# Deformable window sums: one product instruction and one matmul batch per slot, where there were two of each

## The chip, the cores and the metric

The program runs on one core of a Trainium2 chip. The metric is the device time of that core in microseconds (us), the median of several executions. Lower is better.

## The reference, cut to what matters

The kernel is a chain of four layers on an input of 16 images, 64 channels and 16x16 pixels, each added back to its input: a focal modulation block (L0), a deformable convolution (L1), a graph layer over 4,096 nodes (L2) and a convolution with binary weights (L3). The change lies in the deformable convolution alone:

```python
value = (xf @ vp_w.T + vp_b).reshape(n, L, G, cg)      # 8 groups of 8 channels
...
sampled = gather(y0i, x0i, (1 - ty) * (1 - tx)) + gather(y0i, x0i + 1, (1 - ty) * tx) \
        + gather(y0i + 1, x0i, ty * (1 - tx)) + gather(y0i + 1, x0i + 1, ty * tx)
out = jnp.einsum('nhwgk,nhwgkc->nhwgc', mask, sampled)
out = out.reshape(n, L, c) @ op_w.T
```

Offsets are small, so each output pixel needs values from a window of 5x5 pixels. The kernel computes, for each of the 25 window positions (a *slot*), a weight per pixel and group, and sums weight times shifted value over the slots. A path for offsets that reach beyond the window stands behind a flag and isn't taken here.

## The kernel before, in words

Partitions hold image and group and column (or channel and group, in other stages), the free dimension holds pixels (PX = 256). All is in float32 in this stage.

The window stage has four kinds of work, on three engines.

- *Folds* (GpSimd, `fold_rows`, L617, and one of VectorE's, L1128). They multiply the hat functions of y and x for one of nine pairs of window row and tap row into a buffer of nine maps, in three instructions of 768 elements each. Order: pairs 2, 1, 3, then 4, 5, 6 interleaved, then 7, 8. Five buffers; a pair that reuses a buffer waits until the slots of the window row that read it are built (`slot_ready`). Between them GpSimd masks hats (L607).
- *Slot builds* (TensorE, `build_slots`, `add_term`, L1504). They sum the fold maps of a slot, shifted by a constant matrix, into one of four slots in PSUM banks 4 to 7, with 64x64 matmuls of 256 columns. A group of two slots is built at once, in two stages. The group of slots 16 and 17 needs the 18th fold.
- *Products* (VectorE, L1151). For each slot the weights in PSUM times the shifted values in SBUF, once for channels 0, 1, 4, 5 of the layout and once for 2, 3, 6, 7: two instructions (`hh`) of 4 x n elements a partition. n is 224, 240 or 256 pixels, by the window row (slots 0 to 9: 224; 10 to 14 and 20 to 24: 240; 15 to 19: 256). Each goes to one of five ring buffers of 1,024 columns, and waits until the sum that read the buffer is done (`window_added`).
- *Accumulations* (TensorE, `accumulate`, L1490). For each half of a slot, 16 matmuls of 32x32 (4 partition quarters by 4 outputs) with n columns, each with a shift matrix as weights, add the products to banks 0 to 3. A bank holds 256 columns of either half. I call these 16 matmuls a batch.

TensorE's order is written out: the builds of groups 0 and 1, then for each group k the accumulations of its two slots and the build of group k+2. The last group is slot 24 alone. All engines wait on semaphores and run their own streams in order. Ahead of the stage TensorE makes the 27 maps (`pointwise`, L1352) and VectorE turns them (`turn_maps`, L1116). `chunk_of` says which channel lies where, and rules the order in which the weights of the output projection are loaded (`raw2`) and the copy out of the path that isn't taken.

Of the kernel before, what the change touches and what calls it, by code (L numbers as in the profile page):

```python
# [28 lines left out]
P = 128  # L29
# [15 lines left out]
def bass_preact_convs(nc, x, toep3, toep5, toep7, toepd, pw0, pw1, pw2, bias_n, small_x, key_b,  # L45
# [4 lines left out]
    with ctx:  # L50
# [8 lines left out]
        def dram(t, off, dims):  # L59
            return bass.AP(t.tensor, t.offset + off, [list(d) for d in dims])  # L60
# [46 lines left out]
        def cut(lo, n):  # L107
            assert lo + n <= ARENA
            return arena[:, lo:lo + n]
# [38 lines left out]
        dN = turns[:, 0:FULL]  # L148
        omN = [turns[:, FULL:2 * FULL], turns[:, 2 * FULL:3 * FULL]]

        ring = [turns[:, 2304 + c * 1024:3328 + c * 1024] for c in range(3)] + [cut(19968, 1024), cut(6912, 1024)]
        RING, SLOTS, ROW = len(ring), 25, 5
        GROUPS = [(s, s + 1) for s in range(0, 24, 2)] + [(24,)]
        A = sb("A", 3 * PX)

# [58 lines left out]

        def chunk_of(i, j):

            return 4 * ((i ^ j) // 2) + (i ^ j) % 2

        def terms(s, swapped):

# [94 lines left out]
        def slow_vector(dve):  # L315
# [67 lines left out]
            for i in range(4):  # L383
                for j in range(4):
                    ins = dve.tensor_scalar(view(ps, i * 512, [(PX, 2), (1, PX)], 32 * j, 32),
                                            view(acc, chunk_of(i, j) * PX, [(2 * PX, 2), (1, PX)], 32 * i, 32), 1.0, None,
                                            ALU.mult)
            ins.then_inc(sem("window_sum"), 1)
            dve.wait_ge(sem("window_sum"), 1)
# [40 lines left out]
        @block.sync  # L430
        def _(sp):
            load_images(sp, (0, 1), 0)
            load_images(sp, (0, 1), 1)
            load_images(sp, (0, 1), 2)
            load_images(sp, (0, 1), 3)
            sp.dma_start(band5, dram(toep5, 0, [(640, P), (1, 640)])).then_inc(sem("band5_in"), 16)
            sp.dma_start(sN, dram(bias_n, 0, [(13, 32), (0, 4), (1, 13)])).then_inc(sem("bias_in"), 16)
            sp.wait_ge(sem("wt_zero"), 1)
            bands(sp, wt3, toep3, 3, "wt3_in")
            sp.wait_ge(sem("wt_zero"), 2)  # L440
            bands(sp, wt7, toep7, 7, "wt7_in")
            sp.dma_start(sX, dram(small_x, 0, [(SX_N, 8), (0, 16), (1, SX_N)])).then_inc(sem("smallx_in"), 16)
            sp.wait_ge(sem("keyb_zero"), 1)
            sp.dma_start(keyb[0:64, :], dram(key_b, 0, [(0, 64), (1, 1)])).then_inc(sem("small_in"), 16)
            sp.dma_start(rowN[0:16, :], dram(row_n, 0, [(0, 16), (1, 12)])).then_inc(sem("small_in"), 16)
            sp.dma_start(v2raw[0:32, :], dram(v2_w, 0, [(8, 8), (64, 4), (1, 8)])).then_inc(sem("small_in"), 16)
            for gp in range(2):
                for c4hi in range(2):
                    sp.dma_start(view(turned_x, SX_N * c4hi, [(1, SX_N)], 64 * gp, 64),
                                 dram(small_x, 4 * c4hi * SX_N, [(SX_N, 4), (0, 16), (1, SX_N)])  # L450
                                 ).then_inc(sem("turned_in"), 16)
            for p, row in turned_rows:
                sp.dma_start(raw1[p:p + 16, :], dram(pw1, row * 640, [(640, 4), (0, 4), (1, 640)])
                             ).then_inc(sem("raw1_in"), 16)
            for c in range(2):
                sp.dma_start(rawv[:, 64 * c:64 * c + 64],
                             dram(pw1, 256 + 320 * c, [(640, 32), (0, 4), (1, 64)])).then_inc(sem("rawv_in"), 16)
            sp.wait_ge(sem("wt_zero"), 3)
            bands(sp, wtd, toepd, 3, "wtd_in")
            sp.dma_start(alphaT[:, :], dram(alpha, 0, [(0, 2), (1, 64)])).then_inc(sem("l3_in"), 16)  # L460
            sp.dma_start(wraw, dram(sign_w, 0, [(0, 2), (576, 64), (1, 576)])).then_inc(sem("l3_in"), 16)
            for swap, t in enumerate(bias_rows):
                for c4 in range(C4):
                    sp.dma_start(t[32 * c4:32 * c4 + 32, :], dram(bias_n, (c4 ^ (2 * swap)) * 104, [(0, 32), (1, 104)])
                                 ).then_inc(sem("map_bias_in"), 16)
            for j in range(4):
                for i in range(4):
                    p, row = 32 * j + 8 * i, 8 * i + chunk_of(i, j)
                    sp.dma_start(raw2[p:p + 8, :], dram(pw2, row * 128, [(2 * 128, 2), (0, 4), (1, 128)])
                                 ).then_inc(sem("raw2_in"), 16)  # L470

            sp.wait_ge(sem("x2_ready"), 2)
            sp.wait_ge(sem("x2_kept"), 2)
            for c4 in range(C4):
                sp.dma_start(nat(scratch_x2, c4), quad(xs, c4)).then_inc(sem("x2_out"), 16)
            sp.wait_ge(sem("x2_out"), 64)

            sp.dma_start(x2R, dram(scratch_x2, 0, [(64, P), (8192, 32), (1, 64)])).then_inc(sem("x2R_in"), 16)

            sp.wait_ge(sem("HM"), 4)  # L480
            sp.wait_ge(sem("MH"), 4)
            for t in (HM, MH):
                sp.dma_start(t[:, 4096:6144], t[:, 0:2048]).then_inc(sem("wrap_in"), 16)
            for i, q in enumerate((2, 3, 0, 1)):
                sp.wait_ge(sem("y_ready"), i + 1)
                sp.dma_start(dram(out, q * 65536, [(PX, P), (32768, 2), (1, PX)]),
                             view(yout, q * 512, [(PX, 2), (1, PX)])).then_inc(sem("y_out"), 16)
            sp.wait_ge(sem("y_out"), 64)
# [416 lines left out]
        def _(dve):  # L905
# [213 lines left out]
            turn_maps(0, 0)  # L1119
            turn_maps(0, 1)  # L1120
            turn_maps(1, 0)
            for hh in range(2):
                dve.memset(view(ring[hh], 0, [(PX, 4), (1, 2 * HW)]), 0.0).then_inc(sem("ring_zero"), 1)
            turn_maps(1, 1)
            turn_maps(2, 0)
            dve.wait_ge(sem("masked"), 1)
# [8 lines left out]
            for p in range(SLOTS):  # L1135
                by = ROWS[p // ROW]
                if p == 12:
                    dve.wait_ge(sem("over"), 2)
                    dve.tensor_reduce(oversum, over[:, 0:2], AX.X, ALU.add).then_inc(sem("over_rows"), 1)
                dve.wait_ge(sem("slot_ready"), p + 1)  # L1140
                if p == 21:
                    dve.wait_ge(sem("over_all"), 1)
                    dve.tensor_scalar(flag[0:1, :], bank(5)[0:1, PX:PX + 1], 0.0, None, ALU.is_gt).then_inc(sem("flag"), 1)
                y0, n, dy = inside(by)
                for hh in range(2):
                    m = 2 * p + hh
                    if m == RING - 1:
                        dve.wait_ge(sem("maps_turned"), 16)
                    if m >= RING:
                        dve.wait_ge(sem("window_added"), m - RING + 1)  # L1150
                    dve.tensor_tensor(out=view(ring[m % RING], y0, [(512, 2), (PX, 2), (1, n)]),  # L1151
                                      in0=view(values_x, 2 * hh * PX + y0 + dy, [(4 * PX, 2), (PX, 2), (1, n)]),
                                      in1=view(slot(p), y0, [(0, 2), (0, 2), (1, n)]), op=ALU.mult).then_inc(sem("window_prod"), 1)
            dve.wait_ge(sem("flag"), 1)
            far = dve.value_load(flag[0:1, 0:1], min_val=0, max_val=1)
            dve.wait_ge(sem("window_added"), 2 * SLOTS)
            with dve.If(far == 1):
                dve.wait_ge(sem("folded"), 3 * (len(FOLDS) - 1))
                slow_vector(dve)
# [188 lines left out]
        def _(pe):  # L1348
# [130 lines left out]
            values(1)  # L1479
            pe.wait_ge(sem("dw_bias"), G)  # L1480

            def accumulate(p, hh):

                bx = p % ROW
                pe.wait_ge(sem("window_prod"), 2 * p + hh + 1)
                w = ident if bx == 2 else shift[bx]
                y0, n, _ = inside(ROWS[p // ROW]) if p else (0, PX, 0)
                for j in range(4):
                    for i in range(4):
                        ins = pe.matmul(view(bank(i), hh * PX + y0, [(1, n)], 32 * j, 32),  # L1490
                                        view(w, 32 * i, [(1, 32)], 32 * i, 32),
                                        view(ring[(2 * p + hh) % RING], PX * (i ^ j) + y0, [(1, n)], 32 * i, 32),
                                        start=(p == 0 and hh == 0), stop=(p == SLOTS - 1 and hh == 1))
                ins.then_inc(sem("window_added"), 1)

            def add_term(s, i, swapped, n, begins):
# [47 lines left out]
            build_slots(0)  # L1544
            build_slots(1)
            pe.wait_ge(sem("maps_turned"), 16)
            pe.wait_ge(sem("ring_zero"), 2)
            for k, group in enumerate(GROUPS):
                for p in group:
                    accumulate(p, 0)  # L1550
                    accumulate(p, 1)
                if 17 in group:
                    pe.wait_ge(sem("over_rows"), 1)
                    pe.matmul(bank(5)[0:1, PX:PX + 1], oversum, ones[:, 0:1], start=True, stop=True).then_inc(sem("over_all"), 1)
# [226 lines left out]
```

## Time and profile before

| what | us |
|---|---|
| median of 3 executions | 313.93 |
| lowest and highest | 312.32, 315.7 |
| span of the profiled execution | 310.8 |
| between median and span | 3.1 |

The span runs from the first to the last instruction of the program; the time of an execution also takes in what lies around it. The time of the profiled execution itself isn't told beside its span, so the difference to the median stands for it. PE is TensorE, PEld its weight loads, DVE VectorE, ACT ScalarE, POOL GpSimd. A matmul in float32 leaves two records and two weight loads in the trace. Ends of matmuls are modelled, so their starts are the safer reading.

### The profile page before, as it was taken

What the parts mean: (1) busy time and instruction counts of PE and PEld (TensorE: products, weight loads), DVE (VectorE), ACT (ScalarE), POOL (GpSimd) and SP (SyncE); (2) the same over time, 40 slices, a digit from 0 to 9 for tenths busy, and PEclk for the clock granted to TensorE, in tenths of its full rate; (3) what the DMA queues carried; (4) which work ended last, traced back from release to release, by engine and by line L of the source; (5) the groups of instructions that cost most, each with busy time, mean ns of one, the idle gap of its engine ahead of it and who ended that gap; (6) DMA issues with size and microseconds to landing.
All of it is one profiled execution on the core that took longest, in us unless ns stands there. A gap on an engine that the chain in (4) does not pass through costs nothing.

```text
span 310.8 us, 8459 instructions
## 1 busy us (share of the span) xinstructions
PE 278.3 (90%) x3482; PEld 167.4 (54%) x3482; DVE 263.7 (85%) x385; ACT 159.2 (51%) x294; POOL 123.5 (40%) x169
## 2 busy tenths in 40 slices
PE   7797999489799999999799989669999999998995
PEld 7446989227554443456465654653443434457662
DVE  8778999897976699999848876985999999999763
ACT  1396322024241999940000004698888988999221
POOL 8302999973800679999994007000000000000000
PEclk9999999889999999999999999799999999999999
DMA  2512110000000000000000000363000000000003
GB/s 91 162 43 62 31 40 6 2 0 0 3 0 0 0 1 2 4 4 4 5 2 4 4 5 0 136 137 135 1 0 0 0 0 0 0 2 2 0 3 135
DMA packets 6648, 7.99 MB, mean 26 GB/s; under 512 B 2260, under 2 KB 4820, under 8 KB 6612
## 3 DMA queue, kind: packets, MB, share of 16 engines
q1 hardware_dynamic: 6148, 6.86, 7.3%
q10 hardware_dynamic: 464, 0.62, 0.6%
q8 instruction: 26, 0.43, 0.5%
q14 instruction: 10, 0.08, 0.1%
HBM read 4.33 MB, written 2.10 MB: 21 GB/s over the span
## 4 chain that ended last, share of the span: by engine, by line
PE 47%; ACT 13%; POOL 12%; DVE 12%; issue 12%; DMA 1%; ACTq 1%; DVEq 0%; POOLq 0%
PE ps L1352 9%; PE ps L1366 9%; POOL arena L617 9%; PE ps L1609 8%; PE ps L1490 5%; PE ps L1504 5%; PE ps L1387 4%; POOL arena L607 3%; ACT arena L891 3%; PE ps L1692 3%; ACT arena L874 2%; DMA xs<-in_x 1%; DVE arena L1267 1%; ACT arena L683 1%; ACT arena L863 1%
## 5 line engine op out<-in xcount | busy, mean ns | idle before, releaser
L1609 PE MATMUL ps<-arena 128*128 (+1 forms) x256 | 63.4, 380 | 6.3 <-ACT arena L874 4.9
L874 ACT ACTIVATE arena<-ps 128x2048 f32<-128x2048 f32 x32 | 60.1, 1878 | 7.7 <-PE ps L1609 7.7
L1609 PEld LDWEIGHTS ps<-arena 128*128 (+1 forms) x256 | 24.3, 97 | 40.6 <-issue 14.1
L1250 DVE TENSOR_TENSOR arena<-arena 128x1024 f32 (+3 forms) x34 | 36.6, 1154 | 4.0 <-ACT arena L874 4.0
L1151 DVE TENSOR_TENSOR turns<-arena,ps 128x896 f32<-128x896 f32 (+2 forms) x30 | 32.6, 1137 | 6.0 <-PE ps L1504 6.0
L617 POOL TENSOR_TENSOR arena<-arena 128x768 f32<-128x768 f32 x18 | 34.6, 1950 | 2.7 <-ACT arena L777 2.4
L1352 PE MATMUL ps<-turns,k 128*128 128x512 f32 x80 | 34.7, 592 | 0.0
L1366 PE MATMUL ps<-arena 64*64 64x240 f32 (+3 forms) x576 | 30.2, 363 | 4.1 <-issue 2.3
L1267 DVE TENSOR_TENSOR arena<-arena 128x1024 f32<-128x1024 f32 (+13 forms) x30 | 32.2, 1153 | 0.3
L1366 PEld LDWEIGHTS ps<-arena 64*64 64x64 f32 x576 | 27.8, 178 | 7.4 <-issue 4.8
L836 ACT ACTIVATE xs<-ps 128x512 f32<-128x512 f32 x2 | 1.2, 600 | 53.4 <-DVE stats L1175 53.4
L1387 PE MATMUL ps<-ident 128*128 128x128 f32 x174 | 24.3, 306 | 1.6 <-POOL ident L508 1.6
L1352 PEld LDWEIGHTS ps<-turns,k 128*128 128x128 f32 x80 | 15.2, 190 | 19.1 <-issue 18.9
L1387 PEld LDWEIGHTS ps<-ident 128*128 128x128 f32 x174 | 23.7, 221 | 2.5 <-POOL ident L508 1.6
L1151 DVE TENSOR_TENSOR arena<-arena,ps 128x896 f32<-128x896 f32 (+2 forms) x20 | 22.1, 1137 | 2.4 <-PE ps L1504 2.4
L1504 PE MATMUL ps<-arena,shift 64*64 64x256 f32 x168 | 21.0, 395 | 2.4 <-POOL arena L617 1.9
L607 POOL TENSOR_TENSOR arena<-arena 128x768 f32<-128x768 f32 x9 | 16.2, 1821 | 17.5 <-ACT arena L783 17.5
L1116 DVE STREAM_TRANSPOSE arena<-ps 128x512 f32<-128x512 f32 x16 | 15.8, 1073 | 6.0 <-PE ps L1352 5.9
L1490 PE MATMUL ps<-turns,shift 32*32 32x240 f32 (+2 forms) x800 | 19.1, 371 | 0.4 <-DVE turns L1151 0.3
L701 ACT ACTIVATE arena<-ps 128x512 f32<-128x512 f32 x12 | 7.1, 597 | 17.2 <-PE ps L1366 17.2
L1504 PEld LDWEIGHTS ps<-arena,shift 64*64 64x64 f32 x168 | 8.2, 131 | 10.9 <-PE ps L1504 4.2
L1490 PEld LDWEIGHTS ps<-turns,shift 32*32 32x32 f32 x800 | 10.9, 103 | 5.9 <-issue 1.9
(238 smaller groups left out, 513.7 us busy)
## 6 DMA issues: line engine op xcount, KB each, us to landing
scratch_x<-xs SPq DMA_DIRECT2D x4, 256.0 KB
arena<-arena SPq DMA_DIRECT2D x2, 512.0 KB, 3.2
out<-arena SPq DMA_DIRECT2D x4, 256.0 KB, 2.1
xs<-in_x SPq DMA_DIRECT2D x8, 64.0 KB
xs<-in_x ACTq DMA_DIRECT2D x8, 64.0 KB
arena<-in_toep SPq DMA_DIRECT2D x8, 56.0 KB, 2.1
arena<-in_toep SPq DMA_DIRECT2D x1, 320.0 KB, 5.4
raw<-in_pw SPq DMA_DIRECT2D x8, 40.0 KB
```

The costliest lines, as they stand in the source:

```text
L607: pool.tensor_tensor(out=v, in0=v, in1=maps_of(MASK, dy), op=ALU.mult).then_inc(sem("masked"), 1)
L617: pool.tensor_tensor(out=view(folds[i % len(folds)], dx * 3 * PX, [(PX, 3), (1, PX)]), in0=view(hy, (by - dy) * W + (dy * 3 + dx) * PX, [( ...
L874: act.activation(E[k], ps[:, (k % 2) * 2048:(k % 2 + 1) * 2048], ACT.Exp, scale=0.5 / SPLIT ** 2, accum_out=rowsum[:, bass.ds(i, 1)]).then ...
L1151: dve.tensor_tensor(out=view(ring[m % RING], y0, [(512, 2), (PX, 2), (1, n)]), in0=view(values_x, 2 * hh * PX + y0 + dy, [(4 * PX, 2), (PX ...
L1250: dve.tensor_tensor(out=cc, in0=cc, in1=E[k][:, lo * P:hi * P], op=ALU.add).then_inc(sem(name), 1)
L1267: dve.tensor_tensor(out=cc, in0=cc, in1=E[k][:, lo * P:(lo + n) * P], op=ALU.add).then_inc(sem(name), 1)
L1352: ins = pe.matmul(dst, w[:, (c2 * nset + s) * P:(c2 * nset + s + 1) * P], view(src, h * 1024 + c2 * PX, [(512, 2), (1, PX)]), start=(c2 == ...
L1366: ins = pe.matmul(view(bank(b0 + i), y0 * HW, [(1, (y1 - y0) * HW)], 64 * j, 64), weights(slot, dy + r, i), view(src, slot * PX + (y0 + dy ...
L1387: ins = pe.matmul(bank(b, P), ident, ident, start=True, stop=True)
L1490: ins = pe.matmul(view(bank(i), hh * PX + y0, [(1, n)], 32 * j, 32), view(w, 32 * i, [(1, 32)], 32 * i, 32), view(ring[(2 * p + hh) % RING ...
L1504: return pe.matmul(slot(s, 64 * j, 64), view(w, 64 * i, [(1, 64)], 64 * i, 64), view(folds[f % len(folds)], col * PX, [(1, PX)], 64 * i, 6 ...
L1609: ins = pe.matmul(bank(b0 + q), w, m[:, bass.ds(i * P + 512 * q, 512)], start=(t == 0), stop=(t == 1 and q > 0))
```

## The change

The two halves of a slot become one. VectorE writes the products of all eight channels in one instruction of 8 x n elements. TensorE's batch covers both halves: each of the 16 matmuls reads two runs of n columns, one from either half of the buffer, and writes two runs of n columns into its bank. The ring has three buffers of 2,048 columns: one in `turns`, one of two pieces in `arena` that lie 13,056 columns apart, and one in `k1`, the weights of the pointwise matmuls of this layer. The channel order becomes 0 to 3 and 4 to 7.

```diff
-        ring = [turns[:, 2304 + c * 1024:3328 + c * 1024] for c in range(3)] + [cut(19968, 1024), cut(6912, 1024)]
-        RING, SLOTS, ROW = len(ring), 25, 5
+        RING_AT = ((turns, 2304, 1024), (arena, 6912, 13056), (k1, 0, 1024))
+        RING, SLOTS, ROW = len(RING_AT), 25, 5
+
+        def products(p, c, n_c, y0, n, p0=0, n_p=P):
+
+            t, col, step = RING_AT[p % RING]
+            return view(t, col + c * PX + y0, [(step, 2), (PX, n_c), (1, n)] if n_c > 1 else [(step, 2), (1, n)], p0, n_p)
...
-            return 4 * ((i ^ j) // 2) + (i ^ j) % 2
+            return i ^ j
...
-                    sp.dma_start(raw2[p:p + 8, :], dram(pw2, row * 128, [(2 * 128, 2), (0, 4), (1, 128)])
+                    sp.dma_start(raw2[p:p + 8, :], dram(pw2, row * 128, [(4 * 128, 2), (0, 4), (1, 128)])
...
-            for hh in range(2):
-                dve.memset(view(ring[hh], 0, [(PX, 4), (1, 2 * HW)]), 0.0).then_inc(sem("ring_zero"), 1)
+            dve.memset(products(0, 0, 4, 0, 2 * HW), 0.0).then_inc(sem("ring_zero"), 1)
...
-                for hh in range(2):
-                    m = 2 * p + hh
-                    if m == RING - 1:
-                        dve.wait_ge(sem("maps_turned"), 16)
-                    if m >= RING:
-                        dve.wait_ge(sem("window_added"), m - RING + 1)
-                    dve.tensor_tensor(out=view(ring[m % RING], y0, [(512, 2), (PX, 2), (1, n)]),
-                                      in0=view(values_x, 2 * hh * PX + y0 + dy, [(4 * PX, 2), (PX, 2), (1, n)]),
-                                      in1=view(slot(p), y0, [(0, 2), (0, 2), (1, n)]), op=ALU.mult).then_inc(sem("window_prod"), 1)
+                if p == 1:
+                    dve.wait_ge(sem("maps_turned"), 16)
+                if p >= RING:
+                    dve.wait_ge(sem("window_added"), p - RING + 1)
+                dve.tensor_tensor(out=products(p, 0, 4, y0, n),
+                                  in0=view(values_x, y0 + dy, [(4 * PX, 2), (PX, 4), (1, n)]),
+                                  in1=view(slot(p), y0, [(0, 2), (0, 4), (1, n)]), op=ALU.mult).then_inc(sem("window_prod"), 1)
...
-            def accumulate(p, hh):
+            def accumulate(p):
 
                 bx = p % ROW
-                pe.wait_ge(sem("window_prod"), 2 * p + hh + 1)
+                pe.wait_ge(sem("window_prod"), p + 1)
...
-                        ins = pe.matmul(view(bank(i), hh * PX + y0, [(1, n)], 32 * j, 32),
+                        ins = pe.matmul(view(bank(i), y0, [(PX, 2), (1, n)], 32 * j, 32),
                                         view(w, 32 * i, [(1, 32)], 32 * i, 32),
-                                        view(ring[(2 * p + hh) % RING], PX * (i ^ j) + y0, [(1, n)], 32 * i, 32),
-                                        start=(p == 0 and hh == 0), stop=(p == SLOTS - 1 and hh == 1))
+                                        products(p, i ^ j, 1, y0, n, 32 * i, 32),
+                                        start=(p == 0), stop=(p == SLOTS - 1))
...
                 for p in group:
-                    accumulate(p, 0)
-                    accumulate(p, 1)
+                    accumulate(p)
```

## Rows read from the trace of the kernel before

**Rows 1.** The page, first part: busy us, share of the span, instructions.
```profile
PE 278.3 (90%) x3482; PEld 167.4 (54%) x3482; DVE 263.7 (85%) x385; ACT 159.2 (51%) x294; POOL 123.5 (40%) x169
```
**Rows 2.** The chain that ended last, 118 to 186 us: start, us, what.
```profile
138.34 12.06 POOL arena L617 x7
...
154.55 2.40 PE ps L1504 x30
...
175.73 2.58 PE ps L1490 x119
...
179.60 3.79 PE ps L1490 x172
```
**Rows 3.** GpSimd's timeline: start, us, engine, line, operation, shapes.
```profile
138.34 16.07 POOL L617 TENSOR_TENSOR arena<-arena 128x768 f32<-128x768 f32 x9
```
**Rows 4.** VectorE's timeline, memsets and products; in brackets idleness before, and releaser.
```profile
103.49 0.31 DVE L1123 MEMSET turns<- 128x128 f32 x2
104.95 2.00 DVE L1116 STREAM_TRANSPOSE arena<-ps 128x512 f32<-128x512 f32 x2 [1.15 <-PE ps L1352]
...
120.56 3.07 DVE L1151 TENSOR_TENSOR turns<-arena,ps 128x896 f32<-128x896 f32 x3
123.54 2.08 DVE L1151 TENSOR_TENSOR arena<-arena,ps 128x896 f32<-128x896 f32 x2
...
159.41 1.22 DVE L1151 TENSOR_TENSOR turns<-arena,ps 128x1024 f32<-128x1024 f32 x1 [4.58 <-PE ps L1504]
...
175.78 1.15 DVE L1151 TENSOR_TENSOR arena<-arena,ps 128x960 f32<-128x960 f32 x1 [1.31 <-PE ps L1504]
...
180.04 2.21 DVE L1151 TENSOR_TENSOR arena<-arena,ps 128x960 f32<-128x960 f32 x2
```
**Rows 5.** Stretches, L1490 alone: window, us, PE busy, PEld busy, clock, DMA, GB/s.
```profile
139.90:142.60 2.70, 2.54 (x128) 1.78 (x128) 1.00 0.02 6
...
169.90:172.80 2.90, 2.75 (x128) 1.86 (x128) 1.00 0.00 0
175.60:178.40 2.80, 2.65 (x128) 1.85 (x128) 1.00 0.02 6
179.50:183.60 4.10, 3.86 (x192) 2.90 (x192) 1.00 0.02 4
```
**Rows 6.** Line L1490: ns min/median/max, first and last start, form.
```profile
L1490 PEld LDWEIGHTS ps<-turns,shift x800: 101/104/107, 121.9 to 181.6; 32*32 32x32 f32 x160
```
**Rows 7.** TensorE's timeline: the last pointwise matmuls, and the build of slots 8 and 9.
```profile
111.62 7.03 PE L1352 MATMUL ps<-turns,k 128*128 128x512 f32 x16
...
134.02 1.39 PE L1504 MATMUL ps<-arena,shift 64*64 64x256 f32 x12
```
**Rows 8.** Groups by line and shape, 120 to 184 us: busy us, mean ns, idle before.
```profile
L1151 DVE TENSOR_TENSOR turns<-arena,ps 128x896 f32<-128x896 f32 x12 | 12.3, 1086 | 0.0
...
L1151 DVE TENSOR_TENSOR turns<-arena,ps 128x1024 f32<-128x1024 f32 x6 | 7.1, 1217 | 5.6 <-PE ps L1504 5.6
```
**Rows 9.** Stretches, all engines: window, us, busy PE, PEld, DVE, ACT, POOL, PEclk.
```profile
56.90:60.40 3.50, 0.22 (x1) 0.08 (x1) 3.36 (x7) 0.00 (x0) 3.50 (x17) 1.00 0.02 5
60.40:63.80 3.40, 3.33 (x6) 1.46 (x6) 3.30 (x6) 1.74 (x3) 2.90 (x5) 0.51 0.00 0
...
80.00:82.30 2.30, 0.01 (x2) 0.04 (x3) 2.30 (x4) 0.69 (x1) 2.22 (x2) 1.00 0.00 0
...
152.90:154.50 1.60, 0.00 (x0) 0.00 (x0) 1.60 (x2) 0.00 (x0) 1.60 (x2) 1.00 0.04 10
...
193.90:196.00 2.10, 0.00 (x0) 0.00 (x0) 1.95 (x8) 1.21 (x5) 0.00 (x0) 1.00 0.22 85
...
197.00:200.40 3.40, 3.40 (x19) 3.40 (x18) 3.00 (x10) 2.26 (x7) 0.00 (x0) 0.50 0.52 187
```
**Rows 10.** Stretch of the build of slots 16 and 17, L1504 alone, columns as rows 5.
```profile
154.50:159.40 4.90, 4.77 (x60) 2.87 (x60) 1.00 0.00 0
```
**Rows 11.** Line L1504: ns min/median/max, first and last start, form.
```profile
L1504 PEld LDWEIGHTS ps<-arena,shift x168: 129/133/133, 118.6 to 179.0; 64*64 64x64 f32 x168
```

More of the change, by code:

```diff
@@ L385, in slow_vector @@
                     ins = dve.tensor_scalar(view(ps, i * 512, [(PX, 2), (1, PX)], 32 * j, 32),
-                                            view(acc, chunk_of(i, j) * PX, [(2 * PX, 2), (1, PX)], 32 * i, 32), 1.0, None,
+                                            view(acc, chunk_of(i, j) * PX, [(4 * PX, 2), (1, PX)], 32 * i, 32), 1.0, None,
                                             ALU.mult)
@@ L1144, in _ @@
                 y0, n, dy = inside(by)
-                for hh in range(2):
-                    m = 2 * p + hh
-                    if m == RING - 1:
-                        dve.wait_ge(sem("maps_turned"), 16)
-                    if m >= RING:
-                        dve.wait_ge(sem("window_added"), m - RING + 1)
-                    dve.tensor_tensor(out=view(ring[m % RING], y0, [(512, 2), (PX, 2), (1, n)]),
-                                      in0=view(values_x, 2 * hh * PX + y0 + dy, [(4 * PX, 2), (PX, 2), (1, n)]),
-                                      in1=view(slot(p), y0, [(0, 2), (0, 2), (1, n)]), op=ALU.mult).then_inc(sem("window_prod"), 1)
+                if p == 1:
[5 more added lines that the diff above has]
+                                  in1=view(slot(p), y0, [(0, 2), (0, 4), (1, n)]), op=ALU.mult).then_inc(sem("window_prod"), 1)
             dve.wait_ge(sem("flag"), 1)
             far = dve.value_load(flag[0:1, 0:1], min_val=0, max_val=1)
-            dve.wait_ge(sem("window_added"), 2 * SLOTS)
+            dve.wait_ge(sem("window_added"), SLOTS)
             with dve.If(far == 1):
@@ L1546, in _ @@
             pe.wait_ge(sem("maps_turned"), 16)
-            pe.wait_ge(sem("ring_zero"), 2)
+            pe.wait_ge(sem("ring_zero"), 1)
             for k, group in enumerate(GROUPS):
                 for p in group:
-                    accumulate(p, 0)
-                    accumulate(p, 1)
+                    accumulate(p)
                 if 17 in group:
```

## The prediction

> **What bounds the kernel now.** I read the page first, for the share of each engine [rows 1]; TensorE leads with 90%, VectorE follows with 85%, but a share says nothing of the stage that is changed. So the second view is the chain of work that ended last, cut to the window stage [rows 2]. The reader is to see two halves there. Up to 154.4 us the chain lies on GpSimd; its timeline [rows 3] shows nine folds end to end from 138.34 us, 1.79 us each, the last of which TensorE needs for slots 16 and 17. From 154.55 us to 183.39 us the chain lies on TensorE alone, slot builds (L1504) and accumulations (L1490) in turn. VectorE's timeline [rows 4] shows the other side: products back to back at first, 4.58 us of idleness before slot 16 and 1.31 us before slot 22, each time for TensorE. So before 154.5 us the work of VectorE and TensorE has a cover, the folds; only the stretch from 154.5 to 183.4 us can shorten the kernel. The stages behind it follow one from another, so what the window stage gains or loses is passed on.
>
> **The change part by part.** *TensorE's sums.* Today a slot takes two batches of 16 matmuls of n columns; after it one batch of 16 with 2n columns. The matmuls halve (800 to 400; the trace has two records and two weight loads for each), the columns stay. The price of a batch comes from the busy spans of whole groups [rows 5]: six batches of n=240 take 3.86 us and four take 2.65 us, so one takes 0.605 us. Four of n=256 take 2.75 us and four of n=224 take 2.54 us: 0.21 us over 4 x 32 columns, 1.64 ns a column. So a batch of 240 is 0.39 us of columns and 0.21 us that does not grow with them. [...] A batch of 480 columns should take 0.79 + 0.21 = 1.00 us where two took 1.21: 0.21 us less per slot. [...] The nearest row for a moving operand of two runs is the pointwise matmul of 128x512 [rows 7]: 16 of them span 7.03 us, less the last one's 0.59 us over 15 steps 0.43 us each, 1.68 ns a column for the two records of a matmul; two runs cost nothing extra there. I take 0.21.
>
> [...]
>
> *What it is worth on the chain.* Three groups of batches stand in TensorE's order between the folds and slot 23: slots 14/15, 16/17, 18/19. Six slots by 0.21 us: slot 23 is ready 1.26 us sooner than today's 175.7 us. From there VectorE sets the pace: the products of slots 22, 23 and 24, six halves that begin at 175.78 and end at 182.25 us [rows 4]. The means by shape are 1086 ns for 896 elements and 1217 ns for 1024 [rows 8], 1.02 ns an element; started one behind the other they take 2.98 us for three, 0.99 us each, of which 896 x 1.02 = 0.91; the part that does not grow is 0.08 us. Three instructions instead of six save 3 x 0.08 = 0.24 us here (25 over the stage, 2.0 us, the rest covered). Then the end: TensorE ends 1.14 us after VectorE (183.39 against 182.25), and its last batch now has 480 columns where 240 were left: 240 x 1.64 ns = 0.39 us more. Sum: -1.26 - 0.24 + 0.39 = -1.1 us.
>
> Does VectorE become the bound between? Its product of n=256 is 2048 x 1.02 + 0.08 = 2.2 us, two 4.4 us. From slots 18/19 on, TensorE does the batches of 16/17 (2.1 us, and 0.15 for the start of a group), the build of 20/21 (2.2) and the batch of slot 18 (1.05): 5.5 us before it wants product 19. That is 1.1 us of slack. The three double buffers hold more than the five single ones (3 slots against 2.5): product p waits for the sum of slot p-3. Product 21 would start near 171 us and the sum of slot 18 ends near 170 us: 1 us to spare at the nearest ring wait. I cost both at nothing; without that slack they cost what it lacks, once per group.
>
> *The stretch before 154.5 us.* Five groups of two slots (4/5 to 12/13), where TensorE is the one that is waited for, save 5 x 0.42 = 2.1 us, so its sums of slots 12/13 will be done near 150.9 us, not at 152.9. GpSimd gets there at 154.4 us as before: the one slot that it waits for in this stretch, slot 9, is built by 135.4 us today [rows 7], ahead of 138.34. So the gain there is a longer wait of TensorE: 3.65 us instead of 1.65 us.
>
> *The clock.* That wait matters. In this execution the granted clock fell twice within the kernel [rows 9]: at 60.4 us, behind 3.5 us in which TensorE worked 0.22 us, and at 197 us, behind a wait of 2.1 us from 193.9 us on. [...] It did not fall behind the 1.6 us without work at 152.9 us, nor behind the 2.3 us at 80 us. A wait of 3.65 us is longer than each that it outlasted. I expect it to fall here, once, for 3.4 us. What stands there is the build of slots 16 and 17, 4.77 us of dense matmuls [rows 10], all on the chain. At half the clock it loses half of the time that falls into it: 1.7 us if all 3.4 us lie over work, 0.8 us if half of them still lie in the wait. I take 1.3 us; the bounds are 0 (no fall) and 1.7.
>
> [...]
>
> *The rest at nothing.* One memset in place of two, 0.31 us together: VectorE waits 1.15 us behind them for TensorE [rows 4]; without that cover 0.1 us would be won. The output projection's weights come by the same 16 DMAs with another stride, long before use. The third buffer lies in the pointwise weights, whose last use is ahead of the first products; product 1 now has the wait for the turned maps that slot 2's first half had, earlier work of the same engine. The path for far offsets is not run.
>
> **Sum.** -1.1 + 1.3 = +0.2 us on a span of 310.8 us. The median shown is 313.93 us, 3.1 us over the span, which leaves out what lies around the program. So I predict 314.1 us: no change that can be measured. A measurement of this kernel tells about 1% (3.1 us) from nothing; its three runs lie 3.4 us apart.
>
> **Rivals.** (A) *The clock does not fall.* For it: the 2.3 us without a fall. Then only the -1.1 us stand: 312.8 us.
>
> [...]
>
> (C) *The change doesn't do for TensorE what it says:* two runs cost as two matmuls did. Then TensorE saves nothing, its wait stays near 1.65 us, the clock holds, and the later end of the last batch and VectorE's 0.24 us nearly cancel: 314.1 us, by another way than the forecast.
>
> (D) *Slower: a batch of two runs costs more than the two did.* Place: every accumulation from slot 4 on. It decides from 1.21 us per batch of 480 columns. At 1.40 us (0.19 us extra a slot) 21 slots cost 4.0 us, of which the 1.65 us wait for GpSimd absorbs its part, and the last batch's exposed end adds 0.8: +3.1 us, 317.0 us. For it speaks only that no row has a 32x32 tile with two runs, the halves up to 13,056 columns apart; against it the pointwise rows.
>
> **Chances.** Forecast 0.50, A 0.20, B 0.14, C 0.08, D 0.08. Forecast, A, C and B with the fall lie within 1%; B without it comes near the bound, and scatter can carry it over: faster 0.10. D, and a little scatter of the forecast: slower 0.09. Within 1%: 0.81. The range goes from B without a fall (311.5) to the full fall of 1.7 us with the saving cut by 0.5 us (315.1), and 0.1 and 0.5 us beyond for the scatter of a median: 311.4 to 315.6 us.
>
> **What would show it.** Right: 800 records at L1490 with 448 to 512 columns; a group of two batches of 2 x 240 columns busy for 2.2 to 2.3 us; products of 1.9 to 2.2 us; TensorE's wait for the fold before slot 16 at 3.3 to 3.8 us, ending near 154.5 us; the granted clock at 0.5 for 3.4 us right behind it; no waits of VectorE after slot 22. [...] The prediction is wrong at its base if the wait for GpSimd does not end near 154.5 us, or if a ring wait shows up on VectorE.

## The result, and the profile after

The changed kernel took 318.35 us in the median of five executions (314.03 to 318.4) against 314.13 us before (312.32 to 315.7): ratio 1.0111, 95% interval 1.0064 to 1.0158 (the ratio, here and below, is not exactly that of the two medians). It is slower by 1.1% by this ratio and by 1.3% by the medians, where 314.1 us and no change were forecast. Four of the five lie within 0.1 us of 318.35; the fifth, 314.03 us, is the one that was profiled. That already says where to look: the profile shows a kernel of 314 us, and it does not hold what costs the others 4.3 us more.

The page, first part:

```profile
PE 276.2 (88%) x2682; PEld 155.5 (50%) x2682; DVE 261.7 (84%) x359; ACT 159.3 (51%) x294; POOL 124.8 (40%) x169
```

TensorE has 800 matmul records less than in [rows 1]. The groups of batches at the accumulation's line (L1492 now), columns as in [rows 5]:

```profile
147.20:149.60 2.40, 2.24 (x64) 0.81 (x64) 1.00 0.02 7
172.00:174.50 2.50, 2.35 (x64) 0.81 (x64) 1.00 0.00 0
```

A group of two slots takes 2.24 us for n=240 and 2.35 us for n=256, where [rows 5] has 2.65 and 2.75: 0.41 and 0.40 us less, 0.20 us per slot. VectorE's timeline:

```profile
123.48 2.00 DVE L1153 TENSOR_TENSOR turns<-arena,ps 128x1792 f32<-128x1792 f32 x1
125.41 1.99 DVE L1153 TENSOR_TENSOR arena<-arena,ps 128x1792 f32<-128x1792 f32 x1
...
162.33 2.29 DVE L1153 TENSOR_TENSOR arena<-arena,ps 128x2048 f32<-128x2048 f32 x1 [6.23 <-PE ps L1506]
...
177.47 2.15 DVE L1153 TENSOR_TENSOR arena<-arena,ps 128x1920 f32<-128x1920 f32 x1 [1.03 <-PE ps L1506]
...
181.60 2.15 DVE L1153 TENSOR_TENSOR turns<-arena,ps 128x1920 f32<-128x1920 f32 x1
...
185.69 2.51 DVE L1163 STREAM_TRANSPOSE turns<-ps 128x512 f32<-128x512 f32 x4 [1.94 <-PE ps L1492]
```

I call the time from the first product to the first transpose behind the sums the *window stage*. It is 185.69 - 123.48 = 62.21 us here and 184.03 - 120.56 = 63.47 us before: 1.26 us shorter. The chain and TensorE's timeline:

```profile
151.97 5.36 POOL arena L622 x3
...
157.46 2.40 PE ps L1506 x30
...
183.81 1.10 PE ps L1492 x32
```

```profile
157.46 0.43 PE L1506 MATMUL ps<-arena,shift 64*64 64x256 f32 x2 [3.58 <-POOL arena L622]
```

As before the chain goes from GpSimd's folds to TensorE, and the wait between has grown from 1.65 to 3.58 us. Then the clock, all engines, columns as in [rows 9]:

```profile
12.00:15.50 3.50, 3.50 (x5) 1.35 (x4) 2.80 (x9) 1.59 (x3) 0.00 (x0) 0.51 0.38 100
59.90:66.70 6.80, 5.08 (x12) 2.22 (x13) 6.60 (x11) 1.90 (x3) 5.96 (x14) 0.50 0.01 2
83.80:87.20 3.40, 3.40 (x38) 2.70 (x37) 3.23 (x10) 0.59 (x2) 2.56 (x2) 0.50 0.02 5
157.50:160.90 3.40, 3.34 (x50) 2.18 (x54) 0.00 (x0) 0.00 (x0) 3.32 (x2) 1.00 0.00 0
203.20:206.70 3.50, 3.05 (x30) 3.08 (x31) 2.88 (x6) 3.50 (x6) 0.00 (x0) 0.51 0.82 202
```

In this execution the clock did not fall behind the wait. It fell at 12, 60, 84 and 203 us, in stages that the change does not touch; the first three go with a window stage that starts 2.9 us later than in the profile before (123.48 against 120.56), although hardly anything ahead of it was changed. In f1_fill below, which has the same code up to there and whose profile has one fall of 3.4 us in that stretch, it starts at 120.53 us. A single profile of this kernel is one draw of where the clock falls, before as well as after.

### The profile page after: what moved, and what is told of

It is laid out like the page before. It is cut to its first block, busy times and chain, and to the rows that moved or that the text cites. A ratio compares the mean times of both kernels' runs of the same rounds, so it can differ in the third digit from the quotient of the medians.

```text
span 312.3 us, 6833 instructions
## 1 busy us (share of the span) xinstructions
PE 276.2 (88%) x2682; PEld 155.5 (50%) x2682; DVE 261.7 (84%) x359; ACT 159.3 (51%) x294; POOL 124.8 (40%) x169
## 4 chain that ended last, share of the span: by engine, by line
PE 47%; DVE 13%; issue 12%; POOL 12%; ACT 11%; DMA 1%; ACTq 1%; DVEq 0%; POOLq 0%
PE ps L1354 10%; PE ps L1368 9%; POOL arena L622 9%; PE ps L1610 8%; PE ps L1506 4%; PE ps L1389 4%; POOL arena L612 3%; ACT arena L896 3%; PE ps L1693 3%; PE ps L1492 3%; ACT arena L879 2%; PE ps L1590 2%; DVE arena L1269 1%; DMA xs<-in_x 1%; ACT arena L688 1%
## 5 line engine op out<-in xcount | busy, mean ns | idle before, releaser
L1368 PE MATMUL ps<-arena 64*64 64x240 f32 (+3 forms) x576 | 31.8, 377 | 4.1 <-issue 2.3
L1368 PEld LDWEIGHTS ps<-arena 64*64 64x64 f32 x576 | 28.7, 179 | 8.1 <-issue 4.8
L1389 PE MATMUL ps<-ident 128*128 128x128 f32 x174 | 22.4, 291 | 1.6 <-POOL ident L513 1.6
L1153 DVE TENSOR_TENSOR arena<-arena,ps 128x1792 f32<-128x1792 f32 (+2 forms) x8 | 17.0, 2126 | 7.3 <-PE ps L1506 7.3
L1389 PEld LDWEIGHTS ps<-ident 128*128 128x128 f32 x174 | 21.8, 206 | 2.5 <-POOL ident L513 1.6
L1153 DVE TENSOR_TENSOR turns<-arena,ps 128x1792 f32<-128x1792 f32 (+2 forms) x9 | 19.0, 2112 | 1.1 <-PE ps L1506 1.1
L1153 DVE TENSOR_TENSOR k<-arena,ps 128x1920 f32<-128x1920 f32 (+2 forms) x8 | 16.9, 2109 | 0.2
L1354 PE MATMUL ps<-arena 128*128 128x512 f32 x24 | 12.2, 673 | 2.0 <-DVE arena L944 2.0
```

The source lines that it names most:

```text
L1153: dve.tensor_tensor(out=products(p, 0, 4, y0, n), in0=view(values_x, y0 + dy, [(4 * PX, 2), (PX, 4), (1, n)]), in1=view(slot(p), y0, [(0, ...
L1354: ins = pe.matmul(dst, w[:, (c2 * nset + s) * P:(c2 * nset + s + 1) * P], view(src, h * 1024 + c2 * PX, [(512, 2), (1, PX)]), start=(c2 == ...
L1368: ins = pe.matmul(view(bank(b0 + i), y0 * HW, [(1, (y1 - y0) * HW)], 64 * j, 64), weights(slot, dy + r, i), view(src, slot * PX + (y0 + dy ...
L1389: ins = pe.matmul(bank(b, P), ident, ident, start=True, stop=True)
```

## The experiments

Three theories were tested. Theory 1: TensorE's longer wait lets the granted clock fall in most executions, and that costs more than the shorter stage brings. Theory 2: the two-run matmuls or the long products cost time in themselves. Theory 3: the falls in other stages differ by chance. "Median" is of a run's own executions; the kernel before ran beside each set, with medians of 313.98 to 314.14 us. Each run names its mean granted clock per execution. In all 18 profiles of this case the clock stands at 1.00 or at 0.50 and at no other level (values like 0.51, 0.92 or 0.97 are means over a stretch in which it changes), so the mean gives, as an estimate, how much of an execution was at 0.50.

**The changed kernel again** (no edit).

> The changed kernel once more. Theory 1 (clock): the changed window stage is about 1.2 us shorter at full clock, but TensorE's wait for the folds, 3.6 us, lets the granted clock fall in most executions and costs up to 1.7 us there; times near 318.3 us show 2 to 3 more stretches of 3.4 us at 0.5 than the profile of 314.0 us. If the profile falls on such an execution, the fall stands right behind the wait, between 155 and 161 us. Theory 2 (products or two-run matmuls cost more in those executions): the stage from the first product to the last sum is longer than 62 us with the clock at 1.00. Theory 3 (chance): falls lie in other stages than the changed one, and a new set of executions gives times like those of the kernel before, median 314.

Median 316.69 us over 12 executions (312.77 to 318.48), ratio 1.0047 (1.0011 to 1.0083). Its profile is of an execution of 316.87 us:

```profile
152.40:155.90 3.50, 0.00 (x0) 0.00 (x0) 2.18 (x1) 0.00 (x0) 3.50 (x3) 1.00 0.00 0
155.90:157.10 1.20, 1.15 (x23) 0.97 (x25) 0.00 (x0) 0.00 (x0) 1.20 (x1) 1.00 0.00 0
157.10:167.30 10.20, 10.14 (x108) 4.12 (x100) 3.27 (x2) 0.00 (x0) 10.12 (x7) 0.50 0.01 2
167.40:170.80 3.40, 3.33 (x68) 1.73 (x68) 1.15 (x2) 0.00 (x0) 0.90 (x1) 1.00 0.00 0
```

and VectorE's first product and first transpose behind the sums:

```profile
121.96 2.01 DVE L1153 TENSOR_TENSOR turns<-arena,ps 128x1792 f32<-128x1792 f32 x1
...
188.87 2.51 DVE L1163 STREAM_TRANSPOSE turns<-ps 128x512 f32<-128x512 f32 x4 [1.94 <-PE ps L1492]
```

There it is: 3.5 us without a matmul, 1.2 us of work at full clock, then the clock at 0.50 for 10.2 us, though TensorE is busy in nearly all of them (10.14 us). The stage takes 66.91 us, 4.70 us more than the 62.21 us without a fall. Theory 1 holds, with another size than I had given the fall: 4.7 us, where the expectation had up to 1.7. The fall stands where it was expected to begin, and lasts beyond. Theory 2 falls: the stage is longer exactly where the clock is at 0.50. Theory 3 has its part in the scatter (this profile also fell at 58, 82 and 201 us), but not in this stretch.

**A filler in the wait.**

```diff
+                if k == 6:
+                    for _ in range(12):
+                        pe.matmul(view(bank(4), 0, [(1, P)]), ident, ident, start=True, stop=True)
                 if k + 2 < len(GROUPS):
                     build_slots(k + 2)
```

> The changed kernel with 12 matmuls of 128 columns (2.7 us, results unused) in TensorE's order between the sums of slots 12/13 and the build of slots 16/17. Theory 1: no fall behind the wait, 1.3 to 1.7 us less than r1_again in the median, near 312.5 to 316.6 us according to the other falls. Theories 2 and 3: same time as r1_again.

Median 312.76 us (311.0 to 315.91, 12 executions), ratio to the kernel before 0.9954 (0.9923 to 0.9986); 3.9 us under r1_again, where 1.3 to 1.7 us were expected, since the expectation knew only the short fall. TensorE's timeline, and the clock over it (columns as in [rows 9]):

```profile
151.08 2.73 PE L1558 MATMUL ps<-ident 128*128 128x128 f32 x23
154.53 0.43 PE L1506 MATMUL ps<-arena,shift 64*64 64x256 f32 x2 [0.72 <-POOL arena L622]
```

```profile
151.00:157.00 6.00, 5.23 (x58) 4.16 (x58) 2.16 (x1) 0.00 (x0) 5.92 (x4) 1.00 0.01 3
```

The fillers (24 records; the first lies ahead of the view, which starts at 151.3 us) end 0.72 us before the fold arrives, and delay nothing; the clock stays at 1.00; the stage takes 62.23 us. More matmuls and no other edit turn the slower kernel into a faster one. This is the experiment that carries the cause, with d0_delay_before and f0_fill_before below as its controls.

**Half of the change each.** h1_pe_only keeps the two-run batch and the new buffers and splits the product in two instructions; h2_dve_only keeps the long product and splits the batch in two.

```diff
-                dve.tensor_tensor(out=products(p, 0, 4, y0, n),
+                for hh in range(2):
+                    dve.tensor_tensor(out=view(t, col + hh * step + y0, [(2 * PX, 2), (PX, 2), (1, n)]),
...
-                        ins = pe.matmul(view(bank(i), y0, [(PX, 2), (1, n)], 32 * j, 32),
+                        ins = pe.matmul(view(bank(i), hh * PX + y0, [(1, n)], 32 * j, 32),
...
```

> The batch of two runs and the three double buffers, but the products in two instructions of four channels each. Theory 1: TensorE's wait before slots 16/17 as in the changed kernel (3.4 to 3.7 us), so the same falls and times as r1_again, within 0.5 us; six products instead of three at the end cost 0.24 us. Theory 2 with the long product as its cause: back to the time before.

> The product of eight channels in one instruction, but each slot's sums in two batches of n columns (800 matmuls). Theory 1: TensorE has nothing to save, its wait before slots 16/17 is 1.2 to 1.7 us as before the change, no fall there, and the time is that of the kernel before (314 us, within 1 us). Theory 2 with the two-run matmul as its cause: the same. Theory 2 with the long product as its cause: as slow as r1_again.

h1: four executions of 311.16, 316.26, 316.65 and 318.49 us. h2: median 314.71 us, ratio 1.0007 (0.9979 to 1.0036). Their waits before slots 16/17, h1 first:

```profile
159.30 0.43 PE L1508 MATMUL ps<-arena,shift 64*64 64x256 f32 x2 [3.09 <-POOL arena L622]
```

```profile
157.57 0.43 PE L1508 MATMUL ps<-arena,shift 64*64 64x256 f32 x2 [1.29 <-POOL arena L622]
```

The stage takes 62.44 us in h1 and 63.64 us in h2. So TensorE's half of the change is worth 1.03 us and makes the wait; VectorE's half alone is worth nothing on the path (63.64 against 63.47) and has the short wait and the times of before. The six products in place of three at the end, expected at 0.24 us, cost 0.23 us (62.44 against 62.21). Three of h1's four times are as long as r1_again's, but h1 does not show the fall itself: its profile, of the execution of 316.26 us, has the clock at 1.00 behind the wait of 3.09 us, and its falls stand near 11, 28, 62 (6.8 us), 86 and 206 us. The wait in h1 was expected at 3.4 to 3.7 us; it is shorter most likely because VectorE is later with two instructions a slot: its product of slot 12 starts 24.46 us into the stage (149.74 - 125.28), in the changed kernel 23.93 us (147.41 - 123.48).

**The wait without the change.** One more fold on GpSimd, into a scratch tile, in the kernel before.

```diff
+                        if (i, dx) == (4, 1):
+                            pool.tensor_tensor(out=view(A, 0, [(PX, 3), (1, PX)]),
...
```

> The kernel before, with one more fold of 768 elements on GpSimd (result unused) among the folds that slots 16/17 wait for. Theory 1 (a long wait of TensorE lets the clock fall, for up to 10 us, whatever the products look like): the wait grows by the fold's 1.8 us to 3.4 us; most executions fall behind it and lose 4 to 5 us beside the 1.8 us, so the median is 4 to 6.5 us above the kernel before, and the times spread more. Rival (the falls come from the two-run matmuls or the products of eight channels): the 1.8 us alone, 316 us.

Median 317.73 us (317.35 to 320.74, six executions), ratio 1.0130 (1.0078 to 1.0182): 3.6 us over the kernel before, where the fold alone is 1.8 us. The profile has the fall in the kernel of before:

```profile
158.11 0.69 PE L1508 MATMUL ps<-arena,shift 64*64 64x256 f32 x2 [3.45 <-POOL arena L621]
```

```profile
154.70:158.10 3.40, 0.00 (x0) 0.02 (x1) 1.91 (x2) 0.00 (x0) 3.40 (x3) 0.92 0.02 5
158.10:160.90 2.80, 2.79 (x26) 1.80 (x28) 0.00 (x0) 0.00 (x0) 2.72 (x2) 0.50 0.00 0
160.90:164.30 3.40, 3.34 (x49) 1.77 (x49) 0.00 (x0) 0.00 (x0) 3.40 (x3) 0.99 0.00 0
```

Its stage takes 66.64 us: 63.47 + 1.8 + 1.4. So the fall comes with the wait, here of 3.45 us, and not with two-run matmuls, which this kernel does not have. In the profile it is a short one. I had expected 4 to 6.5 us in the median and more scatter; it was 3.6 us, and five of the six times lie within 0.7 us at a mean clock of 0.971 to 0.972.

**A filler in the kernel before,** 6 matmuls in its wait of 1.65 us.

> The kernel before, with 6 filler matmuls (1.3 us) in its wait of 1.65 us before slots 16/17. Theory 1: no fall stood there, so the time of the kernel before within 0.5 us. Rival (filler matmuls help by something else than this fall): faster than before by more than 1 us, as in the changed kernel.

Median 315.34 us (313.35 to 317.99), ratio 1.0035 (0.9995 to 1.0075). The filler brings nothing where no fall stood. The expected "within 0.5 us" is missed to the slow side; in the profile the stage is 64.94 us, and the 1.5 us above 63.47 us stand at its end, where TensorE waits for nothing that the profile shows ("issue").

**The other falls taken away.** Fillers in six waits outside the window stage, near 10, 57, 59, 81, 195 and 202 us, in the kernel before (g_before), the changed one (g_after), and the changed one with the window filler (g_after_fill). The expectation of g_before counts five waits; the edit fills six.

```diff
-            warm_up(25)
+            warm_up(31)
...
+            warm_up(5, 4)
             pe.wait_ge(sem("kmax"), 1)
...
+            warm_up(5, 4)
...
+            warm_up(8, 0)
             pe.wait_ge(sem("x1_ready"), 8)
...
+            warm_up(8, 0)
             for nq in range(NQ):
...
-            warm_up(10)
+            warm_up(18)
```

> The kernel before, with filler matmuls in five waits of TensorE outside the window stage (near 10, 57, 59, 81, 195 and 202 us; 1.1 to 1.8 us each). Theory 1: the falls of the other stages go, the times lie close together and near the lowest seen of the kernel before, 311.5 to 312.5 us. Rival (the spread of the times comes from elsewhere): the same 312.4 to 315.7 us as before.

> The changed kernel with the same fillers, none in the window stage. Theory 1: only the fall behind the wait for the folds is left. In executions with it the kernel is 2 to 4 us slower than g_before, in those without it 1.2 us faster; the median is above g_before. Rival (no fall of its own in the changed stage): 1.2 us under g_before in all.

> The changed kernel with these fillers and the one in the window stage. Theory 1: no fall left; 1.2 us under g_before (what one batch per slot is worth on the chain), with little spread, near 310.8 us. Rival (the change itself costs time at full clock): not under g_before.

| run | median (range), us | ratio (interval) | mean clock of its executions |
|---|---|---|---|
| g_before | 314.79 (314.27 to 316.12) | 1.0046 (1.0015 to 1.0077) | 0.987 to 1.000 |
| g_after | 316.50 (311.76 to 318.50) | 1.0075 (1.0039 to 1.0110) | 0.973 to 0.999 |
| g_after_fill | 312.43 (311.68 to 313.93) | 0.9970 (0.9939 to 1.0001) | 0.988 to 1.000 |

g_before scatters over 1.9 us where the kernel before, in 29 executions beside it, scattered over 5: most of the scatter was falls. But its times are 2 us higher than expected, and its profile, at a clock of 0.999, shows where: 0.8 us behind the window stage (most likely the fillers themselves), and 1.0 us at the end of the stage (64.51 us instead of 63.47):

```profile
PEld ps L1493 <- issue: 1.3, 2, 0.9
```

That row is of 178 to 186 us: TensorE's own weight loads wait 1.3 us for nothing shown, where the kernel before has 0.4 us in the same view. g_after and g_after_fill don't have it. So the difference of 2.5 us between g_before and g_after_fill at full clock is not the change's worth alone. The stages without that stall give it: 62.25 us in g_after_fill against the 63.47 us of the kernel before. g_after_fill was expected near 310.8 us and is 1.6 us above it in the median, 0.9 us in its fastest execution.

Between g_after and g_after_fill only the filler in the window stage differs, and it takes 4.1 us off the median. g_after's profiled execution (311.76 us, clock 0.999) had no fall in the stage:

```profile
150.90:154.40 3.50, 0.00 (x0) 0.00 (x0) 2.21 (x2) 0.00 (x0) 3.50 (x3) 1.00 0.00 0
154.40:157.80 3.40, 3.29 (x46) 2.18 (x50) 0.00 (x0) 0.00 (x0) 3.32 (x2) 1.00 0.02 5
```

Three others took 316.37 to 316.52 us at a clock of 0.984. A mean that is 0.016 under full speed stands for 10.1 us at 0.50 in 315 us, and 311.76 us and the 4.70 us of r1_again are 316.46 us: this fits a long fall, by an estimate, since none of the three was profiled.

**g_after again, and two controls.** n_g_after2 and n_g_after3 are g_after's code again.

> g_after once more, for a profile of an execution of about 316.5 us. Theory 1: one fall, behind the wait for the folds, for 10.2 us, and a window stage of 66 to 67 us; nothing else at half clock before the end. Rival: the time above g_after's profiled 311.8 us comes from another stage.

> The same as n_g_after2, since the place of the wait against the clock's falls varies from execution to execution: the stage is either 62.2 us (no fall) or longer by what the fall takes, 1.5 to 5 us.

n_g_after2: median 316.68 us (312.38 to 318.58), ratio 1.0031 (0.9981 to 1.0081). n_g_after3: 315.04 us (311.79 to 318.28), ratio 1.0027 (0.9987 to 1.0067). n_g_after3's profile:

```profile
151.60:155.20 3.60, 0.01 (x1) 0.01 (x1) 2.23 (x2) 0.00 (x0) 3.60 (x3) 0.97 0.00 0
155.30:158.40 3.10, 3.10 (x28) 1.91 (x29) 0.00 (x0) 0.00 (x0) 3.02 (x2) 0.50 0.02 5
158.40:161.80 3.40, 3.34 (x52) 1.81 (x64) 0.17 (x1) 0.00 (x0) 3.40 (x3) 1.00 0.00 0
```

Both profiles (313.7 and 312.3 us of span) have the short fall: it begins while TensorE still waits (the clock is 0.97 over the wait), lasts 3.4 us, and the stage takes 63.76 and 63.80 us, 1.6 us more than without; the 10.2 us and 66 to 67 us expected of n_g_after2 were missed. So behind a wait of 3.6 us there are three outcomes for the changed stage: no fall (after, g_after), a short one (1.6 us: n_g_after2, n_g_after3), a long one (4.7 us: r1_again, the one profile that has it). Over the 28 executions of g_after, n_g_after2 and n_g_after3 three have the time and the clock of an execution without it (311.76, 311.79, 312.38 us); 17 took 315.4 us or more, as with a long fall or with more than one short one (n_g_after2's profile is of 315.42 us and has three short ones). The rival for n_g_after2 (another stage) holds in part: it also fell at 27 and 68 us.

> g_before with the 6 filler matmuls at 10 us left out. If the stall of 1 us at the end of the window stage goes, executions with a clock of 0.99 or more take 313.0 to 313.5 us, 1.2 us over g_after_fill's 311.7 to 312.0; if it stays, 314.3 us as g_before.

Median 315.17 us (313.84 to 316.38), ratio 1.0039 (1.0013 to 1.0064); at a clock of 1.00 its executions took 313.84 and 314.19 us. The stage is 63.97 us: half of the stall is gone, half of it is still there. The missed 0.5 us stay open.

> g_after_fill with 5 filler matmuls in place of 12 in the window stage, so a wait of 2.4 us is left. Theory 1: as behind the 2.3 us at 80 us, a fall in some executions, in fewer than in g_after (10 of 12) and more than in g_after_fill (none): median between 312 and 314 us.

Median 312.44 us (311.79 to 316.47), ratio 0.9974 (0.9939 to 1.0008). With 2.29 us of waiting left, four of ten executions lie at 313.9 us or more, with a clock of 0.984 to 0.988; with the full wait 24 of the 28 above do, with 0.7 us left (g_after_fill) one of twelve does (313.93 us). Where the falls of the four stood was not seen; the one profile, of 311.8 us, has none, and its stage takes 62.24 us.

**Folds moved to VectorE.** Of the 18 folds that slots 16/17 wait for, VectorE makes two, behind its product of slot 13; in the changed kernel (m1_folds_after), in the kernel before (m0_folds_before), and in the first with the outer fillers (g_m1).

```diff
+                        if (i, dx) in ((6, 1), (6, 2)):
+                            continue
...
+                if p == 14:
+                    dve.wait_ge(sem("masked"), 6)
+                    dve.wait_ge(sem("hats_x"), 2)
+                    for dx in (1, 2):
+                        dve.tensor_tensor(out=view(folds[1], dx * 3 * PX, [(PX, 3), (1, PX)]),
...
+                        if row == 3 and dx:
+                            pe.wait_ge(sem("fold_dve"), dx)
```

> The changed kernel with two of the 18 folds that slots 16/17 wait for moved from GpSimd to VectorE, behind its product of slot 13. Theory 1: GpSimd is through 3.6 us sooner, VectorE with its two folds (1.4 us each) near the same time, TensorE's wait shrinks from 3.6 to 0.5 to 1.0 us, no fall there; the stage takes 59.3 to 59.8 us instead of 62.2, the median is near 310 us. Rival (the folds are not what slots 16/17 wait for): stage as long as before the move.

> The kernel before with the same two folds moved. Theory 1: TensorE itself is done with slots 12/13 only near 153 us, so 1.6 us at most are won, stage near 61.9 us, median 312 to 312.5 us; the step from this to m1_folds_after (2 us or more) is what one batch per slot is worth when nothing covers it.

m1: median 310.35 us (308.76 to 311.78), ratio 0.9874 (0.9827 to 0.9922): it beats both kernels. m0: median 314.78 us, ratio 1.0015 (0.9985 to 1.0045): nothing won. VectorE's timeline of m1, and TensorE's:

```profile
151.82 3.58 DVE L1154 TENSOR_TENSOR arena<-arena 128x768 f32<-128x768 f32 x2
```

```profile
155.55 0.43 PE L1516 MATMUL ps<-arena,shift 64*64 64x256 f32 x2 [1.59 <-DVE arena L1154]
```

The wait of 3.6 us is now 1.59 us, and for VectorE: its folds take 1.8 us each beside GpSimd's, not the 1.4 us of the expectation. The stage takes 60.22 us, 2.0 us less than the changed kernel. In m0 it takes 63.24 us, 0.23 us less than before, not the 1.6 us expected: VectorE reaches its two folds later there and takes 3.80 us for them, and TensorE waits for them. Taken together: with the folds moved, the change is worth 3.0 us of stage (63.24 to 60.22), because what is saved ahead of slot 16 now counts: VectorE reaches its two folds 28.3 us into the stage (151.82 - 123.56), in m0 29.8 us (152.37 - 122.57).

> m1_folds_after with the fillers outside the window stage: a candidate that beats both kernels. 2.5 us under g_after_fill by the shorter wait for the folds, near 308.5 us, and 1.5 to 2 us under m1_folds_after's median of 310.35 us.

Median 310.12 us (309.73 to 310.51), ratio 0.9903 (0.9867 to 0.9940). The stage is 60.20 us, the scatter of its six executions 0.8 us. It is as fast as m1 within the scatter, not 1.5 us faster. The outer fillers take most falls away (its profile has one, near 66 us) and put a cost of their own in place: behind the start of the first transpose the program takes 127.30 us, in m1 126.26 us.

## Why the prediction was wrong

- *What bounds the stage*: right. GpSimd's folds up to slot 16, TensorE behind it.
- *TensorE's sums*: 0.21 us per slot forecast, 0.20 measured (2.24 us for the group, forecast 2.2 to 2.3). Rivals C and D fall with it: C would have left the group at the 2.65 us of [rows 5], D above it. Two batches fewer in a group, with the same columns, took 0.41 us off it: so 0.20 us of a batch do not grow with its columns, near the 0.21 us of the prediction's estimate. What they are spent on, no run shows. The range has two terms that no run shows either: its low end, B without a fall at 311.5 us, counts on a larger saving in the batches than the forecast's, and the 0.5 us less of saving at its high end on a smaller one. What the runs showed in their place is the 0.20 us per slot, so B falls as well.
- *The sum at full clock*: -1.1 us forecast, -1.26 us measured. Counted from the start of the build of slots 16/17, slot 22's product starts 1.22 us sooner (20.01 against 21.23 us; forecast 1.26), the last products take 0.19 us less (forecast 0.24), and the end behind them costs 0.16 us more, where 0.39 was forecast: that term was too large. No wait of VectorE in the stage is for a ring buffer; each is for a slot build.
- *The stretch before 154.5 us*: a wait of 3.65 us forecast, 3.58 us measured, ended by the same fold.
- *The clock*: the step that failed. The prediction said "I expect it to fall here, once, for 3.4 us" and "I take 1.3 us; the bounds are 0 (no fall) and 1.7". The mechanism was right and its size was not: the short fall costs 1.6 us (n_g_after2, n_g_after3), but the fall can last 10.2 us, and then costs 4.7 us (r1_again). I took the length of the two falls in the profile before (0.51 and 0.50 for 3.4 us each, [rows 9]) as the length of a fall. The upper bound of 1.7 us rested on nothing but these two rows, and the range was built on it. With 4.7 us in its place the prediction's own sum gives 314.13 - 1.1 + 4.7 = 317.7 us, above the range.
- *The sum of the two*: with -1.26 + 4.7 us the changed kernel is 3.4 us slower in an execution with the long fall and otherwise the same, and 314.13 + 3.4 = 317.5 us. Its 17 executions (the first five and r1_again's twelve) have a median of 317.02 us. The four at 318.3 to 318.4 us fit the profiled execution of their set with a long fall added: 314.03 + 4.7 = 318.7 us, and its mean clock of 0.973 less 0.016 is 0.957, where theirs is 0.955 to 0.957. r1_again's at 317 us have 0.961 to 0.962, and its profile lacks the fall at 12 us. This is an estimate, since none of the four was profiled.
- *The span and the time*: the prediction put 3.1 us between the profiled span and the median down to what lies around the program. Executions of the kernel before with a span of 310.7 to 310.8 us took 312.4 to 312.6 us, so that is 1.7 to 1.8 us. The rest is that the profile before is of a fast execution: its mean clock is 0.987, that of the executions at 314.0 to 314.2 us 0.976 to 0.978. The sum, a difference on the median, does not change by it; but the profile showed two falls outside the last microseconds where the median execution has more.
- *Rival A* (no fall, -1.1 us) is what the profiled execution shows in its window stage, with falls elsewhere.

What stays open: what decides between no fall, a short and a long one. In n_g_after2, n_g_after3 and d0_delay_before it began while TensorE still waited, and was short; in r1_again it began 1.2 us into the work, and was long; in after, g_after and h1_pe_only (waits of 3.58, 3.57 and 3.09 us) none came. Seven profiles, with one long fall, don't make a rule, and how often the long one occurs is known only by the estimates from times and mean clocks. Open is also the stall ("issue") at the end of the stage, which came with fillers in f0_fill_before and g_before.

## What to carry to other kernels

Time saved on an engine ahead of a wait that another engine ends is not worth nothing: on TensorE it can cost more than it saves. Here the stage was 1.26 us shorter at full clock, the wait grew from 1.65 to 3.58 us, and in r1_again, behind 3.5 us without a matmul, the clock stood at 0.50 for 10.2 us, which cost 4.7 us. So when a change makes TensorE faster under a cover, look at how long its wait becomes beside the waits at which the clock fell, and either move work so that the wait goes (here two folds to VectorE, 1.2% under the kernel before) or fill it with matmuls that end before it does (here 0.72 us before; the clock stayed at 1.00, and the median was 312.76 us against 316.69 us). And the length of a fall seen in one profile is no bound; the mean clock of every execution shows what the one profiled does not.

## What was not expected of the hardware

- The granted clock stayed at 0.50 for 10.2 us while TensorE was busy in 10.14 us of them (r1_again), with matmuls of 64x64 and 32x32 tiles in float32. In n_g_after2 and n_g_after3, with the same window stage, it was back after 3.4 us.
- The same code runs with the clock falling in different stages from one execution to the next: the changed kernel's profile fell at 12, 60 (for 6.8 us) and 84 us ahead of the window stage, that of f1_fill, the same code up to there, only at 61 us. With the waits filled the executions lie within 0.8 us (g_m1, six executions) or 2.3 us (g_after_fill, twelve) instead of 5 us.
- Waits of 3.57 and 3.58 us passed without a fall in two profiles (g_after and after): the clock was 1.00 over the wait and behind it in both.
- A VectorE product of two SBUF operands took 1.8 us for 768 elements beside GpSimd's folds (m1_folds_after), 2.3 ns an element, while a window product, with one operand in PSUM, took 2.15 us for 1,920 elements beside the same folds, 1.12 ns an element. Late in the kernel before, where GpSimd has no work, products of two SBUF operands took 1.09 us for 896 elements (L1250), 1.21 ns an element.
- One execution of h2_dve_only, of ten, took 467.1 us at a mean clock of 0.559, so by an estimate nearly nine tenths of it at half clock. It wasn't profiled.
